# Feed-forward on one core: ScalarE rectifies straight into the activations and squares them there, VectorE is left with the normalisations

## What is computed

```python
h = _bitlinear(x, w_fc) + gate * (x @ v.T @ fast_b.T @ u.T)   # 256 -> 1024; the gate's part is folded into the weight ahead of the loop
r = jnp.maximum(h, 0.0)
return _bitlinear(r * r, w_proj)                               # 1024 -> 256
x = x + _layernorm(_L1_ffn_ref(_layernorm(x), ...))
```

## Time and profile before

| what | us |
|---|---|
| median of 3 runs | 7331.46 (7331.29 to 7333.71) |
| the profiled execution's own time | 7333.02 |
| its span, first to last instruction | 7331.7 |
| mean granted clock of PE | 0.932 of full |

### The profile page before, as it was taken

How to read it: one execution, slowest core, us unless ns; L and a number is a source line. 1 busy time by engine, 2 the same in 40 slices (tenths; PEclk the granted TensorE clock), 3 DMA queues, 4 the chain that set the end, 5 groups by cost and what they waited for, 6 DMA issues and landing times. The chain is left out here.

```text
span 7331.7 us, 59882 instructions
## 1 busy us (share of the span) xinstructions
PE 5765.9 (79%) x18532; PEld 3270.0 (45%) x18532; DVE 5713.5 (78%) x6528; ACT 3248.6 (44%) x6479; POOL 4508.0 (61%) x2730
## 2 busy tenths in 40 slices
PE   5778788787787877878778787797877878778787
PEld 4444354443554435534355343553435544455444
DVE  5589964899649996499964998649986599765997
ACT  1166511665126641277412664126741366313663
POOL 3189740897419964199641995429954299443994
PEclk8899998999899998999889998899988999889998
DMA  2011110111101111011110111101111011110111
GB/s 85 17 38 42 36 46 16 41 41 51 30 21 40 42 45 36 15 40 42 45 36 15 43 42 42 45 9 43 42 39 45 12 42 42 40 42 15 44 42 37
DMA packets 238118, 271.64 MB, mean 37 GB/s; under 512 B 144906, under 2 KB 194994, under 8 KB 231860
## 3 DMA queue, kind: packets, MB, share of 16 engines
q1 hardware_dynamic: 237748, 267.25, 11.4%
HBM read 246.13 MB, written 21.07 MB: 36 GB/s over the span
## 5 line engine op out<-in xcount | busy, mean ns | idle before, releaser
L1197 DVE TENSOR_TENSOR_SCAN wk<-ps,wk 128x1024 f32<-128x1024 f32 x1024 | 2317.2, 2276 | 91.1 <-ACT ps L1713 58.8
L1852 POOL TENSOR_TENSOR wk<-wk 128x1024 f32<-128x1024 f32 x1024 | 2380.8, 2358 | 9.2
L1713 ACT ACTIVATE ps<-wk,Aneg 128x255 f32<-128x255 f32 x4096 | 1704.4, 462 | 1165.8 <-DVE wk L1197 1162.0
L1418 PE MATMUL ps<-wk,ident 128*128 128x512 f32 x4096 | 2012.1, 617 | 24.1 <-DVE wk L1217 24.1
L433 POOL TENSOR_SCALAR rstd<-mv 128x4 f32<-128x4 f32 x146 | 35.8, 245 | 2051.1 <-DVE mv L426 2051.1
L1207 DVE TENSOR_TENSOR wk<-wk,ps 128x1024 f32<-128x1024 f32 x856 | 1022.6, 1195 | 4.2 <-issue 3.5
L1418 PEld LDWEIGHTS ps<-wk,ident 128*128 128x128 f32 x4096 | 738.3, 198 | 630.7 <-issue 597.5
L1413 PE MATMUL ps<-wk,sel 112*128 112x256 bf16 x856 | 244.5, 286 | 714.6 <-DVE wk L1207 709.1
L539 POOL TENSOR_TENSOR wk<-wk 128x4096 f32<-128x4096 f32 x64 | 529.7, 8283 | 292.7 <-ACT wk L661 292.7
L1361 PE MATMUL ps<-xnp,inT 128*128 128x256 f32 (+1 forms) x2048 | 586.3, 411 | 133.3 <-ACT wk L1583 69.9
L1361 PEld LDWEIGHTS ps<-xnp,inT 128*128 128x128 f32 x2048 | 386.9, 201 | 494.1 <-DVE wk L1173 193.5
(11 more groups left out here) (192 smaller groups left out, 8039.7 us busy)
## 6 DMA issues: line engine op xcount, KB each, us to landing
wk<-bc_scr SPq DMA_DIRECT2D x256, 512.0 KB, 3.6
wk<-bc_scr SPq DMA_DIRECT2D x56, 384.0 KB, 3.6
wk<-in_wgT SPq DMA_DIRECT2D x8, 1536.0 KB, 6.5
wk<-in_wuT SPq DMA_DIRECT2D x8, 1536.0 KB, 9.6
wk<-in_wdn SPq DMA_DIRECT2D x8, 1536.0 KB, 6.4
wk<-in_x SPq DMA_DIRECT2D x18, 512.0 KB, 4.0
o_scr<-wk SPq DMA_DIRECT2D x64, 128.0 KB, 3.0
wk<-o_scr SPq DMA_DIRECT2D x32, 256.0 KB, 3.3
```

The costliest lines, as they stand in the source:

```text
L1197: V.tensor_tensor_scan(h, in_time(d, flat(decay(m))), h, 0.0, ALU.mult, ALU.add).then_inc(scanned, 1)
L1418: mm = nc.tensor.matmul(bank(j), ident[:], h[:, 2 * j:2 * j + 2, :] .rearrange("p e t -> p (e t)"), start=first, stop=last)
L1713: nc.scalar.activation(decay(m)[:, e, rest(d)], dl[g % 2][:, e, rest(d)], ACT.Exp, scale=Aneg[:, d, e, n:n + 1]).then_inc(dA_done, 1)
L1852: nc.gpsimd.tensor_tensor(hb[n], du[g % 2], col(Bb[j % 2][:, n % NB, :]) .broadcast_to([P, NDI, MC]), ALU.mult).then_inc(dbu, 1)
```

## The change

The buffer `rl` goes. `relu(s)` writes into `r2[c]` directly, and the square becomes a second ACT instruction that reads and writes the same place of `r2`. On ACT, `square(s - 1)` stands behind `relu(s)`, and a chunk's last square behind its last `relu`. All sixteen squares leave DVE's program, so its closing steps follow one another. PE's `up(s)` waits for `relu(s - 2)` in place of `square(s - 2)`; `bit_down` waits for the squares as before. `relu(0)` waits for `du_done` (the former `square(0)` did), `relu(8)` for `gated`, both of the last unit of the state-space block.

```diff
-        rl = area(24 * KB, 2, CH)
...
-                    def square(s):
-                        c, j = FSTEPS[s]
-                        dve.wait_ge(relu_done, s + 1)
-                        if s == 0:
-                            dve.wait_ge(du_done, NU)
-                        nc.vector.tensor_tensor(r2[c][:, j, :], rl[:, s % 2, :], bank(4 + s % 2), ALU.mult)\
-                            .then_inc(sq_done, 1)
...
-                    for s in range(UP_FIRST):
-                        square(s)
                     out_evac(NU - 1)
-                    squares = iter(range(UP_FIRST, NF))
                     dve.wait_ge(out_ev, NU)
                     for name in ("stats0", "apply0", "stats1", "apply1", "stats2", "apply2"):
                         close_step(0, name, 3, 1)
-                        for s in (next(squares, None),):
-                            if s is not None:
-                                square(s)
-                    for s in squares:
-                        square(s)
...
-                    for s in range(NF, 2 * NF):
-                        square(s)
...
                         if s >= 2:
-                            pe.wait_ge(sq_done, s - 1)
+                            pe.wait_ge(relu_done, s - 1)
...
+                    def rectified(s):
+                        c, j = FSTEPS[s]
+                        return r2[c][:, j, :]
+
                     def relu(s):
                         act.wait_ge(h_mm, s + 1)
                         if s == 0:
-                            act.wait_ge(out_mm, NU - 1)
-                        if s >= 2:
-                            act.wait_ge(sq_done, s - 1)
-                        nc.scalar.activation(rl[:, s % 2, :], bank(4 + s % 2), ACT.Relu).then_inc(relu_done, 1)
+                            act.wait_ge(du_done, NU)
+                        if s == NF:
+                            act.wait_ge(gated, NU)
+                        nc.scalar.activation(rectified(s), bank(4 + s % 2), ACT.Relu).then_inc(relu_done, 1)
+                        if s % NF:
+                            square(s - 1)
+                        if s % NF == NF - 1:
+                            square(s)
+
+                    def square(s):
+                        act.wait_ge(relu_done, s + 1)
+                        x = rectified(s)
+                        nc.scalar.activation(x, x, ACT.Square).then_inc(sq_done, 1)
```

## The result

| | us |
|---|---|
| median of 5 runs after | 7294.2 (7291.56 to 7311.26) |
| median of 5 runs of before | 7333.51 (7331.29 to 7333.79) |
| ratio | 0.9953, 95% interval 0.9941 to 0.9964 |
| the profiled execution | 7303.92, span 7302.6 |

The kernel is faster by about 39 us, where 72.6 were forecast, and 7294.2 lies above the range. The runs also lie further apart than before: 20 us between the fastest and the slowest, 2.5 before.

The account below looks back on a forecast made before the run. In the feed-forward's first chunk, DVE's order of work, squares behind closing steps, was taken to hold PE. Gains of 6.72 + 2.75 - 0.39 = 9.08 us per sequence, 72.6 in eight, gave 7259 us, range 7244 to 7287.

Parts of the forecast that it names:

- The six steps: Feed-forward, first chunk: PE's `up(2)` to `up(7)` follow without pause, 6 x 1.75 = 10.51 us.
- the tail: End of each feed-forward chunk: one `relu` and two squares uncovered, 1.80 us in place of 1.41, 0.39 lost per chunk.
- the square: Feed-forward, on ACT: one square of 512 values takes 0.60 us, between 0.52 and 1.04.
- the first contraction: Feed-forward, first chunk: becomes as fast as the second, 14.08 us in place of 16.83.
- The first `up` to the contraction: Feed-forward, first chunk: 17.39 + 1.80 = 19.19 us in place of 25.91, 6.72 gained.
- That last term, 2.75 us: First contraction of the feed-forward: no clock fall behind the 1.80 us pause, so 2.75 us gained per sequence.
- B: Feed-forward contractions: the clock falls in the new pauses; 7281 if at one contraction, 7303 if at both; chance 0.13.
- C: Feed-forward: ACT becomes the bound, slower than before, 7558 by table loads or 7426 by a slow square; chance 0.03.
- D: Feed-forward: the squares were not what held PE, something unseen takes their place; no change, 7331; chance 0.02.
- How the numbers follow: The prediction's closing part: chances, time 7259, allowances for clock falls elsewhere and the square's bounds, range 7244 to 7287.
- one such fall more or less per sequence is 14 us either way: Later stretches, starting some 9 us earlier per sequence: clock falls may come or go, 1.71 us each, 7245 to 7273.
- the sum: Whole kernel: 6.72 + 2.75 - 0.39 = 9.08 us gained per sequence, 72.6 in eight.

Follow-up runs that it names:

- experiment 8: The kernel before, squares still on DVE, but squares 2 to 7 put ahead of the six closing steps, not between them: 7320.37 us, ratio 0.9977.
- Experiment 1: The changed kernel with three idle ACT copies ahead of the last `bit_out` of every sequence: 7278.31 us, ratio to before 0.9924.
- experiment 2: The kernel before with one idle ACT copy of 640 values ahead of the last `bit_out` of every sequence: 7364.58 us, ratio 1.004.
- experiment 7: The changed kernel with PE adding zeros ahead of units' first projections and three spare matmuls ahead of the wait behind the experts: 7276.24 us, ratio 0.992.
- experiment 5: The changed kernel once more, unaltered: 7293.81 us, ratio 0.995.

## Why the prediction was wrong

The feed-forward was right, term by term. The six steps took 10.47 us (forecast 10.51), the tail 1.72 (1.80), the square 0.62 (0.60), the first contraction 14.08 (14.08). The first `up` to the contraction took 19.08 us (19.19). Per sequence 9.27 us were gained (9.08), the fully granted clock behind a pause of 1.72 us included. That last term, 2.75 us, came true in every feed-forward of the six profiles that have the change, 65.0 us each; but its reason was that the new pause is nearest in length to one that passed without a fall, and length alone does not decide, as shown below. To that extent this part was luck. Rivals B, C and D did not happen: both contractions ran at 1.00, ACT's squares hid beside the `up` steps, and PE's releaser ahead of L1507 is ACT. No table load stands between `relu` and square, which no row of before could show. The section "Table sets: the hidden batching unit" of the Trainium skill's page "ScalarE: Activation LUTs" says that cheap functions (relu, copy, identity, abs) are in every set. The trace agrees for `relu`, with no load in its 128 passes; the square is not in that list, and its 128 passes show no load either. The section "Rules for kernel authors" of the same page would have relu and multiplication on VectorE, with a factor that it gives for bf16; here, in f32, the measurement decides, 0.62 us for the square on ACT against 0.69 on DVE, and experiment 8 shows that most of the feed-forward's gain didn't hang on which.

What failed is the step in "How the numbers follow" where falls of the clock elsewhere were priced: "one such fall more or less per sequence is 14 us either way". The mechanism was the right one, and its size was not. The extra falls came several to a sequence, and at one place of three units they stood on DVE's path: 5.5 us in the state-space block and 1.7 us behind the experts, in five of eight sequences of the profile, with 1.6 to 2.1 us more at the start of each of the five, some 45 us in all in place of at most 14. And I took the falls for as likely to go as to come. The trace of before spoke against that: in all eight of its sequences the 48 pauses of 1.7 us ahead of the projections and the eight behind the experts had passed without costing this, so a move could only lose there. I read the row of another short pause, 1.79 us at a clock of 1.00, as a property of a pause of that length. The next rows of the same timeline already spoke against it, with a longer pause, and PE at the full clock behind it as ahead of it:

```profile
768.41 0.28 PE L1413 MATMUL ps<-wk,sel 112*128 112x256 bf16 x1 [2.17 <-DVE wk L1207]
768.53 1.88 PE L1418 MATMUL ps<-wk,ident 128*128 128x512 f32 x4
```

The profile after and experiments 1 and 2 show that length alone does not decide: the same 1.69 us pause is followed by a fall or not according to when it comes. What makes one moment a bad one is not shown here.

Without the losses the sum holds: the profiled span before, 7331.7, less 74.2, is 7257.5. Experiment 1 bears that out: its span, 7277.4, is 19.9 us above it, and 18.9 of that are its eight waits of 2.36 us. The time itself was not reached by any run here; the nearest profile is experiment 7's, with a span of 7270.3.

## What to carry to other kernels

Work that an engine has to do for another should not stand behind its own long steps: look which instruction releases the waiting engine, and what stands ahead of that one in its program. When a change makes a repeated part shorter, everything behind it moves, and pauses of PE that cost nothing may begin to; a small gain should be tested with a microsecond or two of idle time put in, since a kernel that gets faster by waiting has lost something elsewhere. Here, filling a pause of PE with spare matmuls made the time depend less on that, and moving work from another place into it only moved the pause.

## What was not expected of the hardware

Adding 2.36 us of waiting to each sequence made the kernel 16 us faster, and adding 0.63 us to each sequence of the kernel before made it 31 us slower. A pause of 1.69 us of PE was followed by a stretch at a granted clock of 0.63 in one sequence and of 1.00 in the next. The kernel before repeats every 904.3 to 904.6 us and its eight sequences are alike; the changed one's are not, and its runs spread over 20 us, and over 13 in experiment 5, where the five runs of before that were timed with the first spread over 2.5, and the 17 timed with the second over 12.
